# Four query-packing copies on one DMA queue instead of two queues, in a fused decoder layer

## The reference

```python
x = _layernorm(x + _L0_attn_ref(x, ...))
x = _layernorm(x + _L0_xattn_ref(x, ctx_1024, ctx_1024, ...))
x = _layernorm(x + _L0_ffn_ref(x, ...))

# _L0_xattn_ref, H = 16 heads of 8:
Q, K, V = proj(query, Wq, bq), proj(key, Wk, bk), proj(value, Wv, bv)
scores = jnp.einsum('bhqd,bhkd->bhqk', Q, K) * sm_scale
attn = jax.nn.softmax(scores, axis=-1)
ctx = jnp.einsum('bhqk,bhkd->bhqd', attn, V)
out = jnp.einsum('bsd,ed->bse', ctx, Wo) + bo
```

## Time and profile before

| | |
|---|---|
| median of 3 runs | 634.85 us (631.27 to 636.51) |
| the profiled execution's own time | 631.27 us |
| its span, first to last instruction | 629.4 us |
| TensorE busy | 598.6 us (95% of the span) |
| VectorE / GpSimd / ScalarE busy | 497.1 / 479.3 / 449.0 us |
| granted TensorE clock, mean | 0.981 of full |
| DMAs of one group's queries | 6 of 128 KB: 4 on SP's queue, 2 on ScalarE's |

### The profile page before, as it was taken

How to read it: one execution, slowest core, us unless ns; L and a number is a source line. 1 busy time by engine, 2 the same in 40 slices (tenths; PEclk the granted TensorE clock), 3 DMA queues, 4 the chain that set the end, 5 groups by cost and what they waited for, 6 DMA issues and landing times.

```text
span 629.4 us, 31020 instructions
## 1 busy us (share of the span) xinstructions
PE 598.6 (95%) x13344; PEld 438.9 (70%) x13344; DVE 497.1 (79%) x1279; ACT 449.0 (71%) x831; POOL 479.3 (76%) x619
## 2 busy tenths in 40 slices
PE   9999999999999999999999999999999999896574
PEld 6786777777676767777676777777676777574464
DVE  2655677877888888888888888888888888869887
ACT  4536566869687786869687786869788786848542
POOL 5424154898898989899898989899898989977744
PEclk9999999999999999999999999999999999979788
DMA  8103224263665537273555547263655445343500
GB/s 339 62 19 113 79 75 82 76 131 55 138 112 111 104 111 138 86 131 70 138 111 116 102 112 136 86 131 70 146 104 112 104 107 109 111 53 88 103 19 33
DMA packets 116153, 64.87 MB, mean 103 GB/s; under 512 B 94321, under 2 KB 100850, under 8 KB 115890
## 3 DMA queue, kind: packets, MB, share of 16 engines
q1 hardware_dynamic: 113458, 58.71, 42.6%
q10 hardware_dynamic: 2560, 4.20, 1.9%
HBM read 17.27 MB, written 4.19 MB: 34 GB/s over the span
## 4 chain that ended last, share of the span: by engine, by line
PE 71%; ACT 9%; DMA 6%; DVE 4%; SPq 4%; issue 3%; ACTq 2%; POOL 1%; POOLq 0%; DVEq 0%
PE bank L337 15%; PE bank L357 9%; PE bank L327 8%; DMA gT<-gs 4%; PE bank L449 4%; PE bank L318 3%; PE bank L435 2%; ACT qT L577 2%; PE bank L492 2%; PE bank L295 2%; PE bank L284 2%; PE bank L493 2%; PE bank L414 2%; ACT Qh L626 2%; PE bank L512 2%
## 5 line engine op out<-in xcount | busy, mean ns | idle before, releaser
L337 PE MATMUL bank<-Mh,GT 128*32 128x128 f32 x4096 | 129.4, 276 | 0.0
L337 PEld LDWEIGHTS bank<-Mh,GT 128*32 128x32 f32 x4096 | 108.0, 110 | 21.2 <-issue 17.8
L1202 POOL TENSOR_TENSOR gs<-gall,gs 128x512 f16<-128x512 f32 x56 | 66.1, 1200 | 27.8 <-ACT gs L708 27.6
L924 DVE TENSOR_REDUCE mx<-bank 128x8 f32<-128x512 f32 x128 | 79.1, 682 | 9.4 <-PE bank L414 9.3
L671 ACT ACTIVATE PT<-bank 128x512 f32<-128x512 f32 x128 | 64.4, 625 | 26.0 <-PE bank L435 26.0
L327 PE MATMUL bank<-kp,xs 64*128 64x512 f32 x256 | 77.1, 629 | 0.0
L1197 POOL TENSOR_TENSOR gall<-gall,lnr 128x512 f32<-128x512 f32 x56 | 73.3, 1320 | 1.9 <-DVE st L859 1.9
L598 ACT ACTIVATE x<-x,nmr,rstd 128x128 f32<-128x128 f32 x120 | 50.0, 511 | 30.1 <-POOL nmr L1156 30.0
L550 ACT ACTIVATE Cb<-bank 128x512 f32<-128x512 f32 x81 | 48.2, 595 | 25.7 <-PE bank L337 17.6
L550 ACT ACTIVATE GT<-bank 128x512 f32<-128x512 f32 x95 | 50.4, 601 | 20.8 <-PE bank L327 18.1
L1141 POOL TENSOR_TENSOR rstd<-ve,mhalf 128x4 f32<-128x4 f32 x60 | 61.1, 1018 | 5.0
(11 more groups left out here) (203 smaller groups left out, 1531.5 us busy)
## 6 DMA issues: line engine op xcount, KB each, us to landing
xT<-in_xT SPq DMA_DIRECT2D x16, 256.0 KB, 3.1
xs<-in_x_nat SPq DMA_DIRECT2D x16, 256.0 KB, 2.6
cxT<-in_cxT SPq DMA_DIRECT2D x16, 256.0 KB, 3.6
Kp<-Kh SPq DMA_DIRECT2D x32, 128.0 KB, 2.1
pack<-Qh SPq DMA_DIRECT2D x32, 128.0 KB, 2.6
pack<-Qh ACTq DMA_DIRECT2D x32, 128.0 KB, 3.3
pack<-Ql SPq DMA_DIRECT2D x32, 128.0 KB, 2.9
out_y<-yo SPq DMA_DIRECT2D x15, 256.0 KB, 2.4
```

What stands on the lines that cost most here:

```text
L337: m = e.matmul(bk[32 * j:32 * j + 32, tile(g_)], GT[b % 4][:, tile(hh, 32)], Mh[:, tile(hh)], start=True, stop=True)
L924: e.tensor_reduce(to, bank[uses["score", s, i][0]][:, :].rearrange("p (g b k) -> p g b k", g=2, b=4), AX.X, ALU.max).then_inc(emptied("sco ...
L1202: e.tensor_tensor(gs[t % 2][:, 512:1024], g[t][:, :], gs[t % 2][:, 0:512], ALU.subtract).then_inc(s_gl, 1)
```

## The change

ScalarE no longer issues DMAs. All six DMAs of a group's queries are issued by SP in `qpack`, which waits until both halves of `Qh` are written: first `Qh` for r = 0 (both halves), then `Qh` for r = 2, then, when VectorE is done, `Ql`. ScalarE's waits ahead of its two DMAs go too. The number of DMAs, their shapes and the bytes stay.

```diff
@@ act_program, qproj(s)
                 for i in two:
                     half = slice(64 * i, 64 * i + 64)
                     e.activation(slot(Qh, i), bank[uses["qproj", s, 0][0]][half, :].rearrange("p (b n) -> p b n", b=8), ACT.Identity, bias=xbq[half, 0:1]).then_inc(s_qh, 1)
-                p = s % 2
-                if s > 1:
-                    w.wait_ge(*filled("prob", s - 2, 7))
-                w.wait_ge(s_qh, 2 * s + 2)
-                for r in (0, 2):
-                    e.dma_start(Qp[p][4 + r:128:8, :], Qh[64:128, :]).then_inc(s_qp[p], 16)
@@ sp_program, qpack(s)
                 if s > 1:
                     w.wait_ge(*filled("prob", s - 2, 7))
-                w.wait_ge(s_qh, 2 * s + 1)
-                for r in (0, 2):
-                    e.dma_start(Qp[p][r:128:8, :], Qh[0:64, :]).then_inc(s_qp[p], 16)
-                w.wait_ge(*emptied("qproj", s))
-                for i in two:
-                    e.dma_start(Qp[p][4 * i + 1:128:8, :], Ql[64 * i:64 * i + 64, :]).then_inc(s_qp[p], 16)
+                w.wait_ge(s_qh, 2 * s + 2)
+                for r, src in ((0, Qh), (2, Qh), (1, Ql)):
+                    if r == 1:
+                        w.wait_ge(*emptied("qproj", s))
+                    for i in two:
+                        e.dma_start(Qp[p][4 * i + r:128:8, :], src[64 * i:64 * i + 64, :]).then_inc(s_qp[p], 16)
```

## The result

The changed kernel takes 639.3 us (median of 9 runs, 638.28 to 641.73) against 632.36 us before (9 runs, 629.78 to 636.51): ratio 1.0101, interval 1.0073 to 1.0129. It is 1% slower. (The forecast, 631 us, was made from the first three of these nine runs of before, with their median of 634.85 us.) The time lies in the forecast range, 627 to 640, at its very upper end, and on the other side of no change than was forecast. The profiled execution has a span of 635.5 us, 6.1 us above that of before.

A forecast was written before the change was run, and what follows sets the result against it. TensorE was taken to bound the middle, with waits left in TAIL. -3.1 + 2.8 - 3.7 = -4.0 us gave 627.3 us on the profiled execution, 630.9 carried to the median of 634.85, stated as 631; range 627 to 640.

The forecast's parts named there:

- ScalarE (-3.1 us): In the periods: ScalarE freed of issues, transposes 1.1 to 1.2 us earlier, TensorE's wait goes; 0.28 us in 11 periods.
- SP and the scores (+2.8 us): In the periods: Ql is issued 0.97 us later on SP, so the scores wait 0.2 us in each of 14.
- The part that was held to be unknown, the landing: Time from second Ql issue to landing, six in a row: taken as 2.8 us, between 2.5 and 3.4.
- rival B: Scores wait 0.8 us for Ql every period because landing stays 3.4 us: +7.8 us, 642.6 us; chance 0.11.
- three signs of being wrong: Ql's landing does not get shorter, the clock still falls, or a TensorE gap appears at a step not named.
- half sentence of the chances: A stall of SP with six issues in a row, named within the 0.10 chance of over 1% slower.
- TAIL, group 14 (-3.7 us): L306's wait falls from 2.13 to 0.7 us, the clock stays up, and L318 comes 3.7 us earlier.
- second gap of 1.1 us: In TAIL: TensorE waits about 1.1 us more, after 1.5 us of work behind the 0.7 us gap.
- TAIL, group 15 (0): Ql's copy comes 1.0 us later or less, hidden by VectorE's later maxima; without that cover it costs 1.0 us.

The follow-up runs named there:

- five and one: Against the kernel before: groups 14, 15 packed by SP alone, lower half early; groups 0 to 13 move one of ScalarE's two issues to SP; 626.71 us, ratio 0.9881.
- four copies: The whole change with the r = 2 copies of Qh left out, so it does not compute the layer; 626.72 us, ratio 0.9894 to before.
- measurement of the issue by itself: A kernel without the layer, only query-packing copies in four stretches, with and without TensorE matmuls; issues took at most 0.65 us without matmuls, up to 2.4 us beside them.
- TAIL alone: The change made for groups 14 and 15 only, groups 0 to 13 packed as before; 630.62 us, ratio 0.9951 to before.
- k3 ahead: The whole change, with TensorE's 0.65 us step k3 of the next group moved ahead of the first half of the scores; 634.86 us, ratio 1.0026 to before.
- second stretch: In the kernel without the layer: rounds of six copies on SP beside small matmuls, which ended early; 9 issues took over 0.8 us.
- third stretch: In the kernel without the layer: six copies a round beside matmuls, two of them on ScalarE; longest issue 1.9 us on SP, 2.2 us on ScalarE.

## Why the prediction was wrong

**ScalarE (-3.1 us): the mechanism holds, but the changed kernel does not show it.** There is no idle time ahead of `gs`, and TensorE has no wait for `gT` from 131 to 520 us. But the forecast let the transposes come 1.1 to 1.2 us earlier, and in the changed kernel they come 0.16 us earlier, 6.76 us behind `Qh` in the median instead of 6.92, because SP is late itself. Their wait is gone there while TensorE, held up at the scores, is later too. Where SP is not late, the mechanism shows: five and one has the transposes at 6.05 us, no wait for them, and periods of 35.19 us (four copies 35.16), from 35.35 before. That is about 2 us in 11 periods and not 3.1. A part of the 3.1 was never the transposes': the waits view of before, 131 to 520 us, has a second row, and one of its two waits, ahead of the scores at 234.2 us, follows an issue of SP of 1.98 us.

```profile
PE bank L414 <- DMA pack<-Ql: 0.5, 2, 0.3
```

**SP and the scores (+2.8 us): this step failed.** It took the four `Qh` issues at 2.49 us and said that "one is issued every 0.6 us". In the period shown they took 3.41, because one of them stalled, and one of six did so in each of the groups 0 to 13. The part that was held to be unknown, the landing, was on the good side: 2.51 us where 2.8 was taken, and 2.6 in the median of the `Ql` copies. With issues of 0.6 us and this landing the scores of this period would not have waited at all. Instead the periods are 35.99 us where 35.10 is possible, 9.8 us in 11, and 2.6 us more were lost ahead of them: 12.4 us in place of 2.8. The waits view has 11.4 of them as waits of the scores for `Ql` (17.5 us in the whole span, less 5.8 and 0.3 in TAIL). The price of rival B was of that size (11.2), but its mechanism, a landing that stays at 3.4 us, was wrong. None of the three signs of being wrong that the prediction named turned up: the landing got shorter, the clock held, and the wait stood at a step that it had named. It was the size of that wait, 0.87 us and not 0.2. The stall of SP when six issues stand in a row was named only in a half sentence of the chances, without a price. The profile of before had a hint of it: its view of line L1304 by itself gives 532, 544 and 1983 ns as the least, the median and the longest of an issue, and the sum used 0.6 us for each. The measurement of the issue by itself shows when it stalls: beside matmuls, with instruction packets as all but the only other traffic, and to an end 0.2 to 0.4 us behind that of a packet. That the packet holds the issue up, and that not a third thing ends both, was not isolated further.

**What two issuers save.** The Trainium skill, page "DMA: Bandwidth & Descriptors", section "Issuing engines are not separate DMA queues", says that a second issuer saves only the sequencer's time. That time, 2 x 0.6 us and a stall, is what the change gave up, and the runs agree. In the periods it stands on the path of the scores, where 0.2 us were free.

**The range.** That 639.3 us still lies in it is luck. Its upper end was set between the forecast and the price of rival B, 642.6 us, and the time fell there by a stall that neither has in its sum.

**TAIL, group 14 (-3.7 us): right.** The gap is 0.70 us (0.7 forecast) and the clock holds. The gap is 1.43 us shorter and L306 to L318 2.55, together 4.0. The forecast had a second gap of 1.1 us ahead of the scores; it is 0.34 us, since two matmuls of L327 stand between L306 and the scores, which it left out:

```profile
557.97 1.12 PE L327 MATMUL bank<-kp,xs 64*128 64x512 f32 x2
```

**TAIL, group 15 (0): right.** The scores wait for 5.8 us instead of 4.8. Yet VectorE's maxima start 24.0 us behind L318 (589.06 against 565.08) where it was 24.6 before (585.04 against 560.45), and VectorE is at work without a wait up to them in both, so the later copy costs nothing up to there.

**The end of TAIL: open.** From the last L318 of the periods to that of TAIL the change is 4.8 us shorter (31.5 against 36.3 us), and at the maxima of group 15 5.4 us. The whole part behind the periods is only 3.3 us shorter, and 3.1 us is what TAIL alone gives. What follows the maxima takes 46.5 us in the changed kernel and 44.3 before; over all ten kernels it is 44.0 to 46.7, and 44.0 is the one with k3 ahead, which has the same TAIL as the change. No experiment here says what sets it.

**Sum.** -3.1 + 12.4 - 3.3 = +6.0 us, against 6.1 between the two spans and -4.0 forecast. The 12.4 is counted from the shortest period of before, 35.10 us, so this adds the differences of the profiles up and is no test of the -3.1.

## What to carry to other kernels

Price a run of DMA issues by the longest duration that the trace has for one, not by the median, when someone waits for the last of them. With two pairs on SP, 2 to 4 of the groups 0 to 13 met a stall; with four in a row it was 11, with six 9 to 14. When issues are moved off a busy engine, look separately at each stage: here the same edit was worth -3 us where ScalarE was on TensorE's path and cost 10 where the copies were, and the best version moved one of two issues to a place where SP was waiting anyway. A short gap of TensorE can cost more than its length, if the clock falls behind it.

## What the runs showed of the hardware

- An issue of a 128 KB copy from SP takes 0.53 to 0.64 us while TensorE is idle (144 of 144, and 68 more behind the matmuls), up to 2.4 us beside matmuls when others of the same queue are outstanding, and 0.53 us beside matmuls when none is (24 of 24).
- Every long issue of SP in the changed kernel (14) and beside the matmuls of the second stretch (9) has an instruction packet of 16 KB under way and ends 0.20 to 0.39 us behind it.
- Of ScalarE's two issues in a row the first takes 0.54 us and the second 0.88 (medians of before; 0.87 in the third stretch without matmuls). A single one takes 0.54 (five and one, 14 issues, the longest 0.61).
- `Ql` lands 2.9 us after its issue in the median with two queues in play and 3.1 us in five and one, and 2.6 us with one queue (the change).
- A gap of 2.1 to 2.3 us of TensorE was followed by 1.2 GHz; a gap of 0.70 us, 2.1 us of work and a gap of 0.34 us were not.
